# Reordering the first three stages of a fused network kernel: projection chunks between score units, three PSUM bank pairs for eight transposed units, and batch 0's chain among independent projections

## What is computed

```python
# block 1: attention over 512 tokens, 16 heads of 16, per batch
qkv = x @ w_qkv.T + b_qkv
logits = q @ k.T / math.sqrt(16)
attn = softmax(logits)
h = (attn @ v) @ w_out.T + b_out
h = concatenate([h, txt], axis=1)            # 512 + 77 = 589 tokens
# block 2: a selective scan on the normalised rows
u = layernorm(h)
xp = u @ x_proj_w.T                          # 64 low-rank, 16 B, 16 C
delta = softplus(xp[:, :64] @ dt_proj_w.T + dt_proj_b)
h_t = exp(delta * A) * h_{t-1} + delta * B * u_t     # 16 states
h = h + sum(h_t * C) + u * D_skip
# blocks 3 to 5: one-of-14 experts, causal attention, two-of-128 experts
```

## Time and profile before

| what | value |
| --- | --- |
| median of 3 runs | 1170.27 us (1169.0 to 1170.85) |
| the profiled execution's own time | 1173.3 us |
| its span | 1171.5 us, 14347 instructions |
| mean granted TensorE clock over the span | 0.849 |
| busy in the span | PE 918.4 us (78%), DVE 762.7 (65%), ACT 443.0 (38%), POOL 204.6 (17%) |
| DVE, row maxima L1682, all 128 | 150.3 us busy, 92.2 us idle ahead of them, waiting for PE L686 |
| PE, scores L686 and L766 | 118.8 and 118.6 us busy |
| ACT, exponentials L1305 | 125.5 us busy |

### The profile page before, as it was taken

How to read it: one execution, slowest core, us unless ns; L and a number is a source line. 1 busy time by engine, 2 the same in 40 slices (tenths; PEclk the granted TensorE clock), 3 DMA queues, 4 the chain that set the end, 5 groups by cost and what they waited for, 6 DMA issues and landing times. The chain is left out here.

```text
span 1171.5 us, 14347 instructions
## 1 busy us (share of the span) xinstructions
PE 918.4 (78%) x4632; PEld 505.3 (43%) x4633; DVE 762.7 (65%) x1351; ACT 443.0 (38%) x822; POOL 204.6 (17%) x248
## 2 busy tenths in 40 slices
PE   7899889978988888975576539999489898529980
PEld 2323432242522434223353239999266666414440
DVE  4802569999799997999899931111366767833325
ACT  1156226952169521783452214444123313302220
POOL 1000000111001100011000142333000023246660
PEclk9989877986879869796686859999699988759995
DMA  3099123987039760487666446665600500229957
GB/s 104 11 334 319 59 83 101 216 197 169 1 110 236 182 155 1 119 217 182 178 205 210 146 154 190 196 199 161 242 1 1 218 22 15 75 81 376 400 206 264
DMA packets 75403, 185.57 MB, mean 158 GB/s; under 512 B 12154, under 2 KB 48717, under 8 KB 72656
## 3 DMA queue, kind: packets, MB, share of 16 engines
q1 hardware_dynamic: 60944, 148.11, 37.9%
q0 software_dynamic: 14400, 36.71, 14.4%
HBM read 124.88 MB, written 43.69 MB: 144 GB/s over the span
## 5 line engine op out<-in xcount | busy, mean ns | idle before, releaser
L1682 DVE TENSOR_REDUCE mxn<-ps 128x2 f32<-128x1024 f32 x128 | 150.3, 1219 | 92.2 <-PE ps L686 92.0
L1733 DVE TENSOR_TENSOR_SCAN hst<-dA,dBu 128x1180 f32<-128x1180 f32 x64 | 166.9, 2608 | 0.5
L1305 ACT ACTIVATE Ph<-ps 128x1024 f32<-128x1024 f32 x128 | 125.5, 1075 | 37.1 <-PE ps L766 36.6
L686 PE MATMUL ps<-Kh,Qh 32*128 32x512 f32 x512 | 118.8, 750 | 16.7 <-DVE mxn L1682 13.2
L766 PE MATMUL ps<-Qh,Kh 32*128 32x512 f32 x512 | 118.6, 732 | 1.9 <-ACT Ph L1305 1.8
L1724 DVE TENSOR_TENSOR dBu<-dtu,bc 128x1180 f32<-128x1180 f32 x64 | 88.1, 1381 | 6.7 <-DMA bc<-bc_dram 6.3
L1619 POOL DMA_DIRECT2D yS<-hC x24 | 20.8, 866 | 409.4 <-DVE hC L1743 409.4
L1743 DVE TENSOR_TENSOR hC<-hst,bc 128x1180 f32<-128x1180 f32 x64 | 86.8, 1362 | 0.0
L2043 DVE TENSOR_TENSOR yo<-ps,b2r 128x256 f32<-128x256 f32 x32 | 13.6, 424 | 105.9 <-PE ps L1020 105.9
L1296 ACT ACTIVATE dA<-delta,acol 128x590 f32<-128x590 f32 x64 | 52.2, 816 | 71.3 <-DVE hst L1733 63.2
L779 PE MATMUL ps<-Ph,Vh 128*32 128x512 f32 x512 | 74.1, 653 | 5.2 <-ACT OT L1309 3.3
(11 more groups left out here) (266 smaller groups left out, 1428.8 us busy)
## 6 DMA issues: line engine op xcount, KB each, us to landing
bc<-bc_dram SPq DMA_DIRECT2D x64, 590.0 KB, 5.1
ring<-in_we SPq DMA_DIRECT2D x16, 2048.0 KB, 14.0
W<-in_w SPq DMA_DIRECT2D x46, 512.0 KB, 4.0
yS<-hC POOLq DMA_DIRECT2D x24, 590.0 KB, 6.9
yodd<-hC POOLq DMA_DIRECT2D x24, 590.0 KB, 7.1
xs_dram<-zeros SPq DMA_DIRECT2D x1, 8224.0 KB, 42.7
xg<-xs_dram SPq DMA_DIRECT2D x16, 514.0 KB, 10.9
ys_dram<-zeros SPq DMA_DIRECT2D x1, 5120.0 KB, 47.6
```

What stands on the lines that cost most here:

```text
L686: m = nc.tensor.matmul(ps[:, banks.start + hh % 2, :], Qh[HR * hh:HR * (hh + 1), hg, P * i:P * (i + 1)], Kh[HR * hh:HR * (hh + 1), hg, :], ...
L1305: nc.scalar.activation(Ph[:, n % 2, 2 * g:2 * g + 2, :], ps[:, turned_banks(b, 2 * n + g), :], ACT.Exp, scale=float(HD) ** -0.5).then_inc( ...
L1682: nc.vector.tensor_reduce(slots32(mxn[:, hg % 2, i, :])[:, 2 * g:2 * g + 2, HD], ps[:, score_banks(b, 2 * u + g), :], AX.X, ALU.max, negat ...
L1733: nc.vector.tensor_tensor_scan(hst[:, k % 2, :, :].rearrange("p c t -> p (c t)"), dA[:, k % 2, :, :].rearrange("p c t -> p (c t)"), dBu[:, ...
```

## The change

Four edits in TensorE's program and what belongs to them on ScalarE and VectorE:

1. `project` and `project_v` are split into parts. In `first_front` one part (one chunk, half a projection) stands behind every unit, where whole projections stood behind units 1 and 2. In batch 0 the turned maxima go to bank 7 instead of 4, and the waits follow the new banks.
2. The first transposed scores of batch 0 wait only for the row maxima that last used their banks, and the last `turn_maxima` of batch 0 comes behind the first transposed unit.
3. Transposed sets 0 to 15 of batch 0 use three bank pairs, later ones two, as before. Batch 1's first score set waits for the exponential that last used (5, 6).
4. The order of `first_chain`: a score set of batch 1 between the turns of head groups 2 and 3; the turn of batch 1's first maxima behind the turned values; head group 3's projections and V moved forward, and score sets of units 5, 6, 8 and 9 apart around them; the step-size projection in two parts. ScalarE's copies of these projections move with them, ahead of the standard deviations and `normalise`; V's copies stand directly behind `softplus`. On VectorE the subtraction comes behind both sets of unit 4, and `step_size` and `input_size` behind units 12 and 13 instead of 10 and 11.

The same instructions are issued on every engine; none is added or removed.

```diff
-        def misc_bank(b):
+        def q_bank(b, hg, which):
+            if b == 0:
+                return 4 if hg else which
+            if b == 1:
+                return 7
+            return gap_bank(hg, which) if hg < QG else 4
+
+        def v_bank(b):
             return 7 if b == 1 else 4
+
+        def turn_bank(b):
+            return 7 if b < 2 else 4
...
-        def turned_sets(b):
-            return 3 if b else 2
+        def turned_set(b, v):
+            return SETS[v % 2] if b == 0 and v >= NU else SETS[v % 3]
 
         def turned_banks(b, v):
-            lo, hi = SETS[v % turned_sets(b)]
+            lo, hi = turned_set(b, v)
             return slice(lo, hi + 1)
+
+        def turned_free(b, v):
+            before = [n for n in range(max(0, v - 3), v) if turned_set(b, n) == turned_set(b, v)]
+            return 2 * NU * b + before[-1] + 1 if before else None
+
+        def last_maxima(b, v):
+            return max(n for n in range(2 * NU) if score_set(b, n) == turned_set(b, v)) + 1
...
+            def project_part(b, hg, which, c):
+                bank = q_bank(b, hg, which)
+                if c == 0:
+                    if hg == 0 and which == 0:
+                        pe.wait_ge(x_in, 16 * (b + 1))
+                        if b == 0:
+                            pe.wait_ge(wq_in, 16)
+                    if b == 0:
+                        if hg == 1 and which == 0:
+                            pe.wait_ge(wq_rest_in, 16)
+                        elif hg:
+                            pe.wait_ge(act_q, 2 * hg + which)
+                    elif b >= 2 and hg < QG:
+                        if 2 * hg + which >= 3:
+                            pe.wait_ge(act_q, 2 * HG * b + 2 * hg + which - 2)
+                    elif which:
+                        pe.wait_ge(act_q, 2 * (HG * b + hg) + 1)
+                    elif b == 1 and hg < QG:
+                        if hg:
+                            pe.wait_ge(act_q, 2 * (HG * b + hg))
+                        else:
+                            pe.wait_ge(dve_q, HG)
+                    else:
+                        pe.wait_ge(dve_q, HG * b + (1 if b == 1 else hg - 1))
+                m = nc.tensor.matmul(ps[:, bank, :], wqk[:, hg, which, c, :], xT[:, c, :], start=(c == 0), stop=(c == KC - 1))
+                if c == KC - 1:
+                    m.then_inc(pe_q, 1)
+
...
+            def project_v_part(b, half, i):
+                if i == 0:
+                    if half:
+                        pe.wait_ge(act_v, 2 * b + 1)
+                    elif b == 0:
+                        pe.wait_ge(act_q, 2 * HG)
+                    else:
+                        pe.wait_ge(dve_q, HG * b + (HG - 2 if b == 1 else HG - 1))
+                for c in range(KC):
+                    m = nc.tensor.matmul(ps[:, v_bank(b), D * i:D * (i + 1)], xT[:, c, P * (2 * half + i):P * (2 * half + i + 1)], wv[:, c, :],
+                                         start=(c == 0), stop=(c == KC - 1))
+                if i == 1:
+                    m.then_inc(pe_v, 1)
...
@@ -675,6 +707,8 @@
                     pe.wait_ge(act_q, 2 * (HG * b + hg) + 2)
                 if freed_by(b, v):
                     pe.wait_ge(dve_max, freed_by(b, v))
+                elif b == 1 and v == 0:
+                    pe.wait_ge(act_p, NU - 1)
                 elif b == 1 and v == 2 * QT + 1:
                     pe.wait_ge(dve_vals, 2)
                 elif b == 1 and v:
...
             def turn_maxima(b, hg):
                 pe.wait_ge(dve_max, 2 * (NU * b + QT * (hg + 1)))
-                if hg == HG - 1:
+                if b < 2 and hg:
+                    pe.wait_ge(dve_q, HG * b + hg)
+                if b == 1:
+                    if hg > 1:
+                        pe.wait_ge(act_v, 2 * b + 2)
+                    else:
+                        pe.wait_ge(act_q, 2 * (HG * b + QG + hg))
+                elif b >= 2 and hg == HG - 1:
                     pe.wait_ge(act_v, 2 * b + 2)
-                elif b < 2:
-                    pe.wait_ge(act_q, 2 * (HG * b + (QG if b and hg == 0 else hg + 2)))
                 for i in range(QT):
-                    m = nc.tensor.transpose(ps[:, misc_bank(b), P * i:P * (i + 1)], mxn[:, hg % 2, i, :], ident[:, :])
+                    m = nc.tensor.transpose(ps[:, turn_bank(b), P * i:P * (i + 1)], mxn[:, hg % 2, i, :], ident[:, :])
...
                     unit_scores(b, u)
                     if i == 0 and hg:
                         turn_maxima(b, hg - 1)
-                    if i in (1, 2):
-                        if hg + 1 < HG:
-                            project(b, hg + 1, i - 1)
-                        else:
-                            project_v(b, i - 1)
-                turn_maxima(b, HG - 1)
+                    if hg + 1 < HG:
+                        project_part(b, hg + 1, i // 2, i % 2)
+                    else:
+                        project_v_part(b, i // 2, i % 2)
...
                 hg, j = n // QT, n % QT
-                if n == 0:
+                if n == 0 and b:
                     pe.wait_ge(dve_max, 2 * NU * (b + 1))
                 if j == 0:
                     pe.wait_ge(dve_q, HG * b + hg + 1)
                 for g in range(2):
                     v = 2 * n + g
                     banks = turned_banks(b, v)
-                    if v >= turned_sets(b):
-                        pe.wait_ge(act_p, 2 * NU * b + v + 1 - turned_sets(b))
+                    if turned_free(b, v):
+                        pe.wait_ge(act_p, turned_free(b, v))
+                    elif b == 0:
+                        pe.wait_ge(dve_max, last_maxima(b, v))
...
                 pe.wait_ge(act_p, 2 * (NU * b + n) + 2)
                 if n == 0:
-                    pe.wait_ge(dve_q, HG * (b + 1))
+                    if b >= 2:
+                        pe.wait_ge(dve_q, HG * (b + 1))
                     pe.wait_ge(act_v, 2 * b + 2)
                 elif j == 0:
...
                     tscores(0, u)
                     if u:
                         weighted(0, u - 1)
+                    else:
+                        turn_maxima(0, HG - 1)
...
                     if u >= 8:
                         scores(1, (u - 8) // 2, u % 2)
                 weighted(0, NU - 1)
-                turn_heads(0, range(HG))
+                turn_heads(0, range(QG))
+                scores(1, 4, 0)
+                turn_heads(0, range(QG, HG))
 
             def first_chain():
-                scores(1, 4, 0)
-                turn_maxima(1, 0)
                 turn_values(0, 0)
                 turn_values(0, 1)
                 scores(1, 4, 1)
+                turn_maxima(1, 0)
                 project_out(0, 0)
                 project_out(0, 1)
-                unit_scores(1, 5)
-                unit_scores(1, 6)
+                scores(1, 5, 0)
+                project(1, 3, 0)
+                scores(1, 5, 1)
+                scores(1, 6, 0)
+                project(1, 3, 1)
+                scores(1, 6, 1)
                 turn_tokens(0, low)
                 unit_scores(1, 7)
                 project_x(0, low)
+                scores(1, 8, 0)
                 turn_maxima(1, 1)
-                unit_scores(1, 8)
-                unit_scores(1, 9)
-                project_dt(0, low)
-                project(1, 3, 0)
+                scores(1, 8, 1)
+                project_dt_part(0, low, 0)
+                scores(1, 9, 0)
+                project_dt_part(0, low, 1)
+                scores(1, 9, 1)
+                project_v(1, 0)
                 unit_scores(1, 10)
-                project(1, 3, 1)
-                unit_scores(1, 11)
-                for u in range(12, NU):
+                project_v(1, 1)
+                for u in range(11, NU):
                     unit_scores(1, u)
                     if u == 12:
                         turn_maxima(1, 2)
-                    elif u in (13, 14):
-                        project_v(1, u - 13)
                 turn_maxima(1, 3)
...
             def first_chain():
                 take_vals(0, 0)
                 take_vals(0, 1)
+                take_q(1, 3, 0)
                 standard_deviations(0)
                 normalise(0)
+                take_q(1, 3, 1)
                 take_u(0, low)
                 take_x(0, low)
                 softplus(0, low)
-                take_q(1, 3, 0)
-                take_q(1, 3, 1)
-                begin_sum(0)
                 take_v(1, 0)
                 take_v(1, 1)
+                begin_sum(0)
                 decay(0, 0)
...
             def first_chain():
-                maxima(1, 4, 0)
+                unit_maxima(1, 4)
                 minus(1, 0)
-                maxima(1, 4, 1)
                 residual(0)
                 moments(0)
                 maxima(1, 5, 0)
@@ -1815,9 +1862,9 @@
                     unit_maxima(1, u)
                     if u % QT == 0:
                         minus(1, u // QT - 1)
```

(25 more changed lines are left out.)

30 lines of the change are left out of this document (3 added, 27 removed).

## The result

| | kernel before | changed kernel |
| --- | --- | --- |
| median, first comparison | 1170.56 us (1169.0 to 1176.1, 4 runs) | 1156.09 us (1153.1 to 1162.7, 4 runs) |
| median, run again (e1 below) | 1170.95 us (33 runs) | 1159.45 us (1154.3 to 1162.4, 10 runs) |
| ratio | | 0.9891 [0.9849, 0.9933]; again 0.9896 [0.9863, 0.9930] |
| profiled execution, its span | 1173.3, 1171.5 us | 1158.53, 1156.7 us |

The change makes the kernel 1.05% faster, some 12 us; the forecast was 8.8. In the two traces the spans differ by 14.8 us, and 12.8 of them are won ahead of the scans (182.0 - 169.2). From the last turn of batch 1's maxima to the end of the span it is 989.5 us before (1171.5 - 182.0) and 987.5 after (1156.7 - 169.2); the traces of e1 to e8, before and changed orders alike, have 987.6 to 990.6 there.

The account below looks back on a forecast made before the run. Hand-overs between TensorE and VectorE bound the front, TensorE the transposed units, no full engine the chain. Heads 4.7 us sooner plus 4.1 in the chain gave 8.8 us: median 1170.27 to 1161.5 us, range 1155.5 to 1166.5.

Parts of the forecast that it names:

- Part 1: Front of batch 0: projection chunks between units shorten the middle head groups from 11.33 to 10.44 us; 4.3 us gained.
- Part 2: Hand-over to transposed units: one pair of score sets goes ahead of the last maxima turn; 3.9 us of the gain arrives.
- the negation is late next: At the hand-over, ScalarE's exponentials still wait for the negation behind VectorE's last subtraction; first exponential at 58.65 us.
- Part 3: Batch 0's transposed units 0 to 7: a third bank pair turns heads 4.7 us sooner, bounds 3.0 and 9.8.
- a stretch as long costs half its length: In the packed transposed units, a low-clock stretch like that of 60.0 to 70.2 us returns and costs 5.1 us.
- Part 4: Batch 0's chain reordered, heads to last turned maxima: 7.1 us gained at full clock, 4.1 after 3.0 for low clock.
- About one of them: In the chain, two holes together cost 3.0 us through low clock, about one stretch; bounds 0 and 6.3.
- the first hole: In the chain, TensorE stands 1.3 us at the values; a low-clock stretch after it would cost 3.4 us.
- the second hole: In the chain, TensorE stands 1.9 us at batch 1's V; low clock there would cost 2.9 us.
- The clock stays high: Rival, chance 0.13: none of the three new holes brings 1.2 GHz; 16.9 us gained, 1153.4 us.
- The slower rival: Rival, chance 0.06: the chain stays at 1.2 GHz from values to softplus; about 14 us lost, about 1184 us.

Follow-up runs that it names:

- e1: The changed kernel again without any edit, with more rounds and a second trace; median 1159.45 us, 0.9896 of the kernel before.
- e8: The kernel before with two unused matmuls in the 2.45-us hole ahead of the last turn of batch 0's maxima; 0.9989 of the kernel before.
- e9: The kernel before again without any edit, for a second trace, on a third chip; ratio 1.0000.
- e6: Changed kernel with old hand-over, two bank pairs and old chain, leaving only the projection chunks and the maxima's new bank; 0.9961 of the kernel before.
- e4: Changed kernel with whole projections behind units 1 and 2 of each head group again, the new bank kept; 0.9923 of the kernel before, median 1161.86 us.
- e2: Changed kernel with batch 0's last turned maxima ahead of the first transposed scores again, which wait for all row maxima; 0.9905 of the kernel before.
- e3: Changed kernel with two bank pairs for all transposed units of batch 0; 0.9945 of the kernel before, median 1163.57 us.
- e7: Changed kernel with one unused matmul in the 1.2-us hole ahead of the turned values; 0.9893 of the kernel before.
- e5: Changed kernel with batch 0's chain in the old order on TensorE, ScalarE and VectorE; 0.9934 of the kernel before.
- e11: Changed kernel with unit 11's scores ahead of the second half of batch 1's V on TensorE; 0.9918 of the kernel before.
- e12: Changed kernel with the small negation ahead of the front, unit 11's scores ahead of V's second half, and an unused matmul before the turned values; 0.9883 of the kernel before.

## Why the prediction was right, and where its terms were off

**Part 1, 4.3 us: right in size, half of it by another mechanism.** At full clock and with the old hand-over it is 4.0 us (47.87 in e9 against 43.91 in e6). The layout came out: one pause a group of 0.75 to 0.80 us where 0.78 was worked out, a group of 10.54 us where 10.44 was. But the prediction puts the gain down to the places of the chunks, "only their places change", and never names the bank. By e4 the places give 2.0 us, and the wait on bank 4 that the new bank of the turned maxima takes away gives the other 2.0. The first exponential, at 58.29 on the old trace's zero (the first scores start at 14.30 instead of 13.63) against a forecast of 58.65, is close partly by luck: the 4.3 from 48.95 to 44.66 hold 1.1 us that the low clock had cost the first trace, less the 0.7 that part 2 lost.

**Part 2: what is late next was named rightly, its price not.** The text says that the negation is late next, but not that two sets ahead of the turn push it back. e2 prices it: 0.74 us lost, where the forecast let 3.9 of part 1's 4.3 arrive, a loss of 0.4.

**Part 3 is the step that failed**, and in one term: "a stretch as long costs half its length, 5.1 us. I take that it comes back". In the seven traces with three pairs and the late negation the stretch lasted 0 us three times, 3.4 three times and 6.8 once, and cost 0, 1.6 or 3.2 us, 1.1 in the mean. The rest of the term stands: 79.2 was forecast for unit 8's scores at full clock, and the trace has 80.03, which is 79.4 on the old zero. The mistake was to read one execution's clock as a property of the kernel; e9, with the same hole, has no low stretch at all. Of the 9.6 us by which the heads moved (107.8 to 98.2 behind the first scores) 4.0 are part 1's with its bank and 2.6 the third pair's, 0.7 were lost by part 2, and 3.8 were the cost of a stretch that the kernel before does not always have (forecast: about 3).

**Part 4: order right to 0.2 us, clock right in kind.** At full clock 35.1 us to softplus's end and 53.5 to the last turn were forecast; e3, e4 and e7 have 35.3 and 53.6. Each hole is where it was put. "About one of them" at 3.0 us: the first hole's stretch costs 3.1 (38.4 against 35.3) and came in four of seven traces; the second hole was never followed by one in the unaltered order. But the 7.1 us count against the 60.6 of the first trace, whose own chain was low for long; e9 takes 57.3. What the order wins at equal clock stays open between 0.9 and 3.7 us (e5).

**The sum.** 8.8 was forecast, 11.5 to 14.5 measured by medians, 12 by the larger sample: against the first trace of before, from which the forecast counts, the two traces of the changed kernel win 13.5 and 11.9 us up to the last turn, and the surplus is the 5.1 of part 3 that came to 0 and 1.6, less part 2's loss. Against e9 they win only 6.4 and 4.8. With two traces of the kernel before, 7 us apart, how much of the 12 us each term gives is not shown beyond the stages, and that the total fell into the range is in part luck. Undone one at a time, the parts cost 0.3% (part 1, the places alone), 0.1 (part 2), 0.5 (part 3) and 0.4 (part 4) of the time, each uncertain by 0.3 to 0.4; the front alone gives 0.4.

**The rivals.** "The clock stays high" is what the first trace shows for the transposed units, not for the chain, which is why 1156.1 lies between its 1153.4 and the forecast's 1161.5. The rule cited there (the Trainium skill, page "TensorE: Matmul & The Clock Gate", section on how HAM oscillation bites in real kernels) warns only of longer holes. Here 1.2 GHz follows the hole of 1.21 us in four traces and not in three, so by these traces the rule does not keep a hole of that length safe; that the hole is the cause is not shown (e7). The slower rival found nothing: in the changed order the chain was low for 6.8 us at most ahead of softplus's end.

## What to carry to other kernels

Lay the order out instruction by instruction with the trace's own hand-over times (here 1.17 us from scores to reduction, 0.85 for a copied operand): that gave each hole to 0.3 us. Take the clock's stretches out of such a sum, give them as a range with bounds from several traces of the same kernel, and get a second trace of before, since the clock of one execution moved a stage by up to 3 us and the stretch to the last turn by 7 (168.4 against 161.3 for the same kernel). When a change moves work and a buffer at once, undo them apart: half of part 1's gain was a bank that was no longer shared. When a stage is moved forward, look for the last small instruction ahead of its consumer on another engine; here a 0.17-us negation set the start, and reordering behind it only delayed it.

## What the runs showed of the hardware that was not expected

- The low stretch behind the same hole differs between executions of the same program. Behind the 2.45-us hole: 10.2 us (before) and 0 (e9). Behind the 0.87-us hole, with the same orders up to there: 0, 3.4, 6.8, 3.4 and 0 us (changed, e1, e5, e7, e11). In the chain 1.2 GHz follows a hole of 1.21 us in four traces of seven. What decides it stays open.
- Low stretches lasted from 3.4 to 23.9 us. In the tail of the changed order (161.4 to 185.2) TensorE was busy 21.3 of 23.8 us and the clock stayed at 1.2 GHz, while VectorE was busy 22.5. What this cost behind the last turn was not measured. At the start of e4 6.8 us at 1.2 GHz follow 3.32 us of idle time and cost 2.6 us.
- The third chip's 1193.2 us for the kernel before, against 1171.0 and 1168.8 on the others, lies behind the stages studied: there it is 1009.1 to 1014.4 us from the last turn to the end in e9 to e12, and 987.5 to 990.6 on the others. Its cause was not looked for.
